# Attention step: all value units of a batch in one run at its end, twelve buffers of exponentials, heads set singly between half projections

## The reference

```python
Q = layernorm(x) @ Wq.T + bq; K = ctx @ Wk.T + bk; V = ctx @ Wv.T + bv
scores = softmax(einsum('bhsd,bhtd->bhst', Q, K) / sqrt(16))
x = x + tanh(g_xattn) * (einsum('bhst,bhtd->bhsd', scores, V) @ Wh.T + bh)
x = x + tanh(g_ffn) * moe_ffn(layernorm(x))   # 8 experts, best 2, low-rank updates, F = 1024
```

## Time and profile before

| what | us |
|---|---|
| median of 3 runs | 541.9 |
| the runs | 544.21, 534.79, 541.9 |
| profiled execution | 535.67 |
| its span, first to last instruction | 533.9 |
| PE busy | 505.6 (95%) |
| DVE, POOL, ACT busy | 355.7, 291.2, 257.9 |
| granted PE clock, mean | 0.99 |

### The profile page before, as it was taken

How to read it: one execution, slowest core, us unless ns; L and a number is a source line. 1 busy time by engine, 2 the same in 40 slices (tenths; PEclk the granted TensorE clock), 3 DMA queues, 4 the chain that set the end, 5 groups by cost and what they waited for, 6 DMA issues and landing times.

```text
span 533.9 us, 11800 instructions
## 1 busy us (share of the span) xinstructions
PE 505.6 (95%) x4358; PEld 460.0 (86%) x4358; DVE 355.7 (67%) x774; ACT 257.9 (48%) x576; POOL 291.2 (55%) x335
## 2 busy tenths in 40 slices
PE   3788999999999999999998999999999999999995
PEld 2576888888888888888788999999999999999993
DVE  6866677777777777887766777765475555754443
ACT  2556565555555555556767523453335334343331
POOL 5552566655554566552559955744367433844441
PEclk9989999999999999999999989999999999999998
DMA  7575687667677777764111000001000100001000
GB/s 212 142 251 123 197 209 151 168 156 161 165 163 169 177 186 190 163 141 110 24 18 15 2 1 1 2 1 31 2 1 1 32 0 1 2 0 32 0 1 31
DMA packets 51287, 45.83 MB, mean 86 GB/s; under 512 B 34295, under 2 KB 40703, under 8 KB 51231
## 3 DMA queue, kind: packets, MB, share of 16 engines
q1 hardware_dynamic: 41324, 21.03, 16.9%
q0 software_dynamic: 6560, 15.83, 12.4%
q10 hardware_dynamic: 3346, 8.23, 5.3%
HBM read 20.59 MB, written 6.66 MB: 51 GB/s over the span
## 4 chain that ended last, share of the span: by engine, by line
PE 80%; DVE 6%; DMA 6%; ACT 2%; SPq 2%; issue 1%; POOL 1%; ACTq 0%; POOLq 0%; DVEq 0%
PE bank L1293 13%; PE bank L1155 9%; PE bank L1185 7%; PE bank L1172 7%; PE bank L1345 6%; PE bank L1297 6%; PE bank L1310 6%; PE bank L1132 5%; PE bank L1140 5%; PE bank L1325 4%; DMA QS<-crow 4%; PE bank L1218 2%; PE bank L1328 2%; DVE nmax L911 2%; PE bank L1259 2%; PE bank L1247 2%
## 5 line engine op out<-in xcount | busy, mean ns | idle before, releaser
L911 DVE TENSOR_REDUCE nmax<-bank 100x1 f32<-100x361 f32 x256 | 128.0, 527 | 52.8 <-PE bank L1155 49.4
L400 POOL TENSOR_TENSOR awl<-hb,awh 128x400 fp32r<-128x400 f32 x64 | 71.2, 1114 | 102.3 <-ACT awh L604 102.3
L509 ACT ACTIVATE pt<-bank 120x400 f32<-120x400 f32 (+1 forms) x192 | 82.7, 505 | 24.2 <-PE bank L1172 23.8
L1155 PE MATMUL bank<-KS,QS 96*100 96x362 f32 x256 | 88.8, 383 | 4.9 <-DVE nmax L911 3.1
L850 DVE TENSOR_TENSOR hb<-sil,bank 128x400 f32<-128x400 f32 x64 | 36.5, 570 | 83.4 <-PE bank L1310 39.1
L604 ACT ACTIVATE awh<-hb 128x400 fp32r<-128x400 f32 x64 | 34.5, 539 | 118.9 <-DVE hb L857 118.6
L343 POOL DMA_DIRECT2D KS<-kn x64 | 33.2, 526 | 90.6 <-PE bank L1155 56.2
L1155 PEld LDWEIGHTS bank<-KS,QS 96*100 96x100 f32 x256 | 42.0, 167 | 23.9 <-issue 13.4
L1172 PE MATMUL bank<-QS,KS 97*120 97x200 f32 (+1 forms) x384 | 50.8, 268 | 2.7 <-DVE qn L760 1.6
L1172 PEld LDWEIGHTS bank<-QS,KS 97*120 97x120 f32 (+1 forms) x384 | 48.9, 185 | 4.9 <-DMA QS<-crow 2.8
L333 POOL DMA_DIRECT2D QS<-q_dram x90 | 46.2, 526 | 6.4 <-DMA q_dram<-qn 6.4
(11 more groups left out here) (178 smaller groups left out, 1123.9 us busy)
## 6 DMA issues: line engine op xcount, KB each, us to landing
KS<-kn SPq DMA_DIRECT2D x128, 90.5 KB, 2.9
KS<-kn POOLq DMA_DIRECT2D x64, 90.5 KB, 2.7
craw<-ctxT POOLq DMA_DIRECT2D x14, 361.0 KB, 5.5
QS<-q_dram POOLq DMA_DIRECT2D x92, 50.0 KB, 5.1
q_dram<-qn ACTq DMA_DIRECT2D x4, 400.0 KB, 4.9
o_dram<-on SPq DMA_DIRECT2D x16, 100.0 KB
xr<-o_dram SPq DMA_DIRECT2D x16, 100.0 KB
y<-xs SPq DMA_DIRECT2D x16, 100.0 KB
```

The costliest lines, as they stand in the source:

```text
L400: nc.gpsimd.tensor_tensor(awl[:, g % 2, slot], hb[:, slot], awh[:, g % 2, slot].bitcast(F32), ALU.subtract).then_inc(m["p_awl"], 1)
L509: nc.scalar.activation(pt[0:TW[t], u % 6, :], pT[u % 3][0:TW[t], 0:CS], ACT.Exp, scale=float(DH) ** -0.5).then_inc(m["act_e"], 1)
L911: nc.vector.tensor_reduce(nmax[:, pos:pos + 1], pS[h % 2][0:S, 0:T], AX.X, ALU.max, negate=True).then_inc(m["dve_s"], 1)
L1155: mm(pS[h % 2][0:S, 0:TP], QS[b % 3][0:96, g, h % 2, j, :], KS[b % 3][0:96, g, j, :], start=True, stop=True).then_inc(m["pe_s"], 1)
```

## The change

- PE: in steps 0 to 14 the twelve value units of batch i come in one run at the end of step i, behind head 15; step 15 keeps its four visits. The visit behind scores 0 to 2 is gone.
- pt has twelve buffers (UN = 12) instead of six; exponential u waits for value unit u of the batch before.
- PE: k_proj and v_proj are cut into halves of three matmuls, with one head between the halves, where heads stood in pairs.
- ACT: row_out(i, 1) goes between exponentials 1 and 2, k_high(b, 0) ahead of the copy of the sums, row_out(i + 1, 0) between exponentials 7 and 8.
- DVE: k_low(b, 0) goes from behind head 4 to behind head 3, k_low(b, 1) from ahead of head 8 to behind it; ctx_high, the small operations root and head 14 move by a place.

```diff
-        pt = sba("pt", [121, 6, CS])
+        pt = sba("pt", [121, UN, CS])
...
-                wait(act, "pe_pv", n - 5)
-                nc.scalar.activation(pt[0:TW[t], u % 6, :], pT[u % 3][0:TW[t], 0:CS], ACT.Exp,
+                wait(act, "pe_pv", n - UN + 1)
+                nc.scalar.activation(pt[0:TW[t], u, :], pT[u % 3][0:TW[t], 0:CS], ACT.Exp,
...
                     expo(i, 1)
+                    row_out(i, 1)
                     expo(i, 2)
+                if has_k(i):
+                    k_high(b, 0)
                 if has_o(i):
                     wait(act, "pe_pv", i * UN)
...
                     head(i + 1, 7)
+                    head(i + 1, 8)
                 if has_k(i):
                     k_low(b, 1)
-                if i in (11, 12):
-                    root(0, 7 * (i - 11) + 2)
-                if has_s(i):
-                    head(i + 1, 8)
...
+            def k_part(b, j, p0, p1):
+                for p in range(p0, p1):
+                    (hw, hc), k = TERMS[p // KT], p % KT
+                    last = mm(pP[(1, 0)[j]][:, 0:TP], wkv[:, 0, hw, k, j * 128:(j + 1) * 128],
+                              cth[:, b % 2, hc, k, :], start=p == 0, stop=p == 5)
+                if p1 == 6:
+                    last.then_inc(m["pe_k"], 1)
...
                     st_unit(i, 2)
-                if has_o(i):
-                    pv_unit(i - 1, 9)
-                    pv_unit(i - 1, 10)
-                    pv_unit(i - 1, 11)
                 if has_s(i):
                     s_head(i + 1, 0)
-                    s_head(i + 1, 1)
...
-                    k_proj(b, 0)
+                    pe.wait_ge(m["ctx_l"], b + 1)
+                    k_part(b, 0, 0, 3)
+                if has_s(i):
+                    s_head(i + 1, 1)
+                if has_k(i):
+                    k_part(b, 0, 3, 6)
                 if has_s(i):
                     s_head(i + 1, 2)
+                if has_k(i):
+                    wait(pe, "act_c", 2 * i + 2)
+                    v_part(b, 0, 0, 3)
+                if has_s(i):
                     s_head(i + 1, 3)
                 if has_k(i):
-                    wait(pe, "act_c", 2 * i + 2)
-                    v_proj(b, 0)
+                    v_part(b, 0, 3, 6)
                 if has_s(i):
                     s_head(i + 1, 4)
...
                     s_head(i + 1, 9)
                 if has_k(i):
                     wait(pe, "dve_kl", KT * b + 2)
-                    v_proj(b, 1)
+                    v_part(b, 1, 0, 3)
                 if has_s(i):
                     s_head(i + 1, 10)
+                if has_k(i):
+                    v_part(b, 1, 3, 6)
...
+                if has_s(i):
+                    s_head(i + 1, 14)
                 if has_y(i):
                     y_proj(i)
                 if has_s(i):
-                    s_head(i + 1, 14)
                     s_head(i + 1, 15)
+                    pv_unit(i, 0)
+                    pv_unit(i, 1)
...
+                    pv_unit(i, 11)
```

More of the change, by code:

```diff
@@ L649, in body @@
                     expo(i, 7)
+                if has_s(i):
+                    row_out(i + 1, 0)
+                if has_u(i):
                     expo(i, 8)
@@ L653, in body @@
                     w_high(5)
-                if has_s(i):
-                    row_out(i + 1, 0)
                 if has_k(i):
@@ L973, in body @@
                     head(i + 1, 2)
-                    head(i + 1, 3)
                 if i in (11, 12):
@@ L977, in body @@
                 if has_s(i):
-                    head(i + 1, 4)
+                    head(i + 1, 3)
                 if has_k(i):
                     k_low(b, 0)
+                if has_s(i):
+                    head(i + 1, 4)
+                if i in (11, 12):
+                    root(0, 7 * (i - 11) + 2)
                 if has_s(i):
@@ L1023, in body @@
                     head(i + 1, 12)
-                    head(i + 1, 13)
                 if i in (11, 12):
                     root(0, 7 * (i - 11) + 5)
+                if has_s(i):
+                    head(i + 1, 13)
+                    head(i + 1, 14)
                 if i == 1:
@@ L1039, in body @@
                 if has_s(i):
-                    head(i + 1, 14)
                     head(i + 1, 15)
@@ L1129, in k_proj, with v_part @@
                     pe.wait_ge(m["ctx_l"], b + 1)
-                for n, (hw, hc) in enumerate(TERMS):
-                    for k in range(KT):
-                        last = mm(pP[(1, 0)[j]][:, 0:TP], wkv[:, 0, hw, k, j * 128:(j + 1) * 128],
-                                  cth[:, b % 2, hc, k, :], start=n + k == 0, stop=n + k == 3)
-                last.then_inc(m["pe_k"], 1)
+                k_part(b, j, 0, 6)
+            def k_part(b, j, p0, p1):
[5 more added lines that the diff above has]
+                    last.then_inc(m["pe_k"], 1)
             def v_proj(b, t):
+                v_part(b, t, 0, 6)
+            def v_part(b, t, p0, p1):
                 bank = pP[1] if b < 2 and t == 1 else pP[0]
-                for n, (hw, hc) in enumerate(TERMS):
-                    for k in range(KT):
-                        last = mm(bank[0:TW[t], 0:D], cth[:, b % 2, hc, k, T0[t]:T0[t] + TW[t]],
-                                  wkv[:, 1, hw, k, :], start=n + k == 0, stop=n + k == 3)
-                last.then_inc(m["pe_v"], 1)
+                for p in range(p0, p1):
+                    (hw, hc), k = TERMS[p // KT], p % KT
+                    last = mm(bank[0:TW[t], 0:D], cth[:, b % 2, hc, k, T0[t]:T0[t] + TW[t]],
+                              wkv[:, 1, hw, k, :], start=p == 0, stop=p == 5)
+                if p1 == 6:
+                    last.then_inc(m["pe_v"], 1)
             def s_head(b, h):
@@ L1422, in body @@
                 b = i + 2
-                if has_u(i):
-                    st_unit(i, 0)
-                    st_unit(i, 1)
-                    st_unit(i, 2)
-                if has_o(i):
-                    pv_unit(i - 1, 9)
-                    pv_unit(i - 1, 10)
-                    pv_unit(i - 1, 11)
+                st_unit(i, 0)
+                st_unit(i, 1)
+                st_unit(i, 2)
                 if has_s(i):
                     s_head(i + 1, 0)
-                    s_head(i + 1, 1)
-                if has_u(i):
-                    wait(pe, "act_v", min(NT * (i + 2), NT * B))
-                    wait(pe, "act_c", 2 * i)
-                    row_turn(i, 1)
-                    if i == B - 1:
-                        gate(0)
+                wait(pe, "act_v", min(NT * (i + 2), NT * B))
+                wait(pe, "act_c", 2 * i)
+                row_turn(i, 1)
+                if i == B - 1:
+                    gate(0)
                 if has_k(i):
@@ L1469, in body @@
                     u_proj(0)
+                if has_k(i):
+                    wait(pe, "act_v", NT * b + 1)
+                    k_part(b, 1, 0, 3)
                 if has_s(i):
@@ L1472, in body @@
                 if has_k(i):
-                    wait(pe, "act_v", NT * b + 1)
-                    k_proj(b, 1)
+                    k_part(b, 1, 3, 6)
                 if i == B - 2:
@@ L1519, in body @@
                     wait(pe, "act_v", NT * b + 2)
-                    v_proj(b, 2)
+                    v_part(b, 2, 0, 3)
                 if has_s(i):
                     s_head(i + 1, 13)
+                if has_k(i):
+                    v_part(b, 2, 3, 6)
+                if has_s(i):
+                    s_head(i + 1, 14)
                 if has_y(i):
@@ L1525, in body @@
                 if has_s(i):
-                    s_head(i + 1, 14)
                     s_head(i + 1, 15)
+                    pv_unit(i, 0)
+                    pv_unit(i, 1)
+                    pv_unit(i, 2)
+                    pv_unit(i, 3)
+                    pv_unit(i, 4)
+                    pv_unit(i, 5)
+                    pv_unit(i, 6)
+                    pv_unit(i, 7)
+                    pv_unit(i, 8)
+                    pv_unit(i, 9)
+                    pv_unit(i, 10)
+                    pv_unit(i, 11)
             for i in range(0, B):
```

41 lines of the change are left out of this document (20 added, 21 removed).

## The result

The change made the kernel slower: a median of 554.59 us in 4 runs (551.36 to 558.62) against 538.39 us for the kernel before in 4 runs (534.79 to 544.21), a ratio of 1.030 with a 95% interval of 1.0245 to 1.0349. The forecast was 536, its range 521 to 550. The profiled execution took 553.36 us, with a span of 551.5 (before: 535.67 and 533.9). My sum had given 532.0 for it, so 21.4 us are missing.

A forecast was written before the change was run, and what follows sets the result against it. PE's own issue time was taken to bound the step: 14.61 - 1.08 + 1.03 = 14.56 us. Together -3.7 us gave 532.0 for the profiled execution; between medians of 532 and 538 the forecast was 536, range 521 to 550.

The forecast's parts named there:

- (d): Store of the row maxima ahead of scores unit 6: taken as landing in time, 0 us, bounds 0 and +1.4 us.
- step 0 at +0.5: First attention step: three visits become a burst, a wait is added and a DVE hole goes, +0.5 us in all.
- (e): Roots in steps 11 and 12, row_out and osb copy change places on engines with slack: 0.3 us for the roots.
- the clock at 1.00: TensorE's granted clock in steps 0 to 14, read from the earlier trace as 1.00, the full 2.4 GHz.
- (a): One visit to the value units for four, in each step: 3.47 us become 2.4, saving 1.08 us a step.
- R3: Rival: a visit's price goes with its units, or 192 records outpace what feeds PE; 544 us, chance 0.1.
- (b): Halves of projections with one head between, on PE: no cost taken, bounds +-0.3 us a step.
- (c): New DVE order: PE waits for the low half of k before the second v projection, 1.03 us in steps 0 to 13.
- R1: Rival: the wait for the low half of k doesn't bite; steps of 13.5 us, 518 to 524 us, chance 0.2.
- way of 0.42 us: PE's time from head 8's matmul to the second v projection before the change, without the visit's tail: 0.42 us.
- R2: Rival: the row store still lands late; 12 to 18 us if in thirteen steps, 544 to 550 us; chance 0.2.
- base of 541.9: Median of the kernel before's runs used by the forecast: 541.9 us, 6.2 us above the profiled execution.

The follow-up runs named there:

- all three repairs: Changed kernel with DVE's low half of k back ahead of head 8, roots 4 and 11 ahead of the context cast, xr load behind the row store: 532.83 us, 0.988.
- the kernel before with two repairs: Kernel before with the xr load behind the row store of step 0 and two roots ahead of the context cast in steps 11 and 12: 535.68 us, 0.989.
- the single repairs: Three runs of the changed kernel, one edit each: low half of k ahead of head 8, 537.81 us; roots ahead of context cast, 546.17; xr load behind store, 546.72.

## Why the prediction was wrong

The undisturbed step was right. What failed are terms beside it that were put at nothing or nearly so: the store at 0 us (d), step 0 at +0.5, the roots at 0.3 (e), and the clock at 1.00. Of the 21.3 us of span above my sum, the holes for the store and the roots are 2.42 + 2.15 + 4.52 = 9.1 us. Half clock is up to 7.9 us by an estimate from the window rows (PE was busy for 15.7 of the 17.0 us at 0.50, and half of that is lost). 2.5 us lie outside the stage, and the rest is spread.

**(a), the burst: right.** 2.4 us were forecast for twelve units, with entry and exit; 2.2 us stand between its start and the next scores. The saving of 1.08 us a step was 0.9 under the new order. R3 is out. What I had not seen is that it holds only with that order; in the old one 0.3 us is left. At first I had read a visit as pure cost, since PE goes on without a hole; but DVE was working under it (the rows of the burst alone show PE waiting for it in its place), and the earlier trace rows had shown DVE busy in three quarters of the time.

**(b), single heads: right within its bounds.** A head between two half projections takes 0.17 to 0.18 us (188.31 to 188.48, 195.35 to 195.53).

**(c), the wait for the low half of k: right in mechanism, place and size.** 1.46 us from head 8 to the v projection against 1.45 forecast, and the third group of the step takes 3.34 us where the sum had 3.08 - 0.81 + 1.03 = 3.30. R1 is out, and the step comes to 14.67 against 14.56. Only the way of 0.42 us without the wait was too short: undoing the order gives back 0.62 us and leaves 0.77, so R1's step of 13.5 us wasn't to be had.

**(d), the store at 0 us: wrong, and R2 was right on it in some steps.** The distance, 6.01 us, was right. Landings of 5.08, 5.47 and 5.36 us cost 0.50, 0.87 and 0.78 us in steps 2, 6 and 8, or 2.1 us. R2's price for late landings in thirteen steps, 12 to 18 us, did not come, so the result above 550 doesn't speak for R2. I had argued that the cause moves away, because the loads of q end earlier. They do, by 0.8 us in step 9: GpSimd has issued them 2.2 us into the step and not 3.0. But the store moves with them, from 2.6 to 1.5 us into the step, so that they end 0.64 us behind its issue where they ended 0.35 us behind it. By its semaphore in the traces it landed after 2.6 to 5.5 us in steps 1 to 11, and after 4.6 to 6.0 before: the moves helped, but not in every step, and the slack of 4.5 us is short by what is left. The Trainium skill, "DMA: Bandwidth & Descriptors", Queues, rings and completion order, says that each DMA engine takes turns between the queue rows, packet by packet. That a small store then waits for its own row and little else was my inference from it, and the rows don't bear it out: alone in ACT's queue the store landed after 5.41 us.

**Step 0 at +0.5 us: wrong, it was +6.0.** The row that I cited for it, 0.29 us for the store at 52.65, was the warning: nothing of the store's lateness could move, since it is issued when those four loads have landed, while PE arrives earlier by as much as the new order shortens the way (from 6.5 to 5.7 us of the step). Each tenth that PE saves ahead of it is a tenth of hole. The store was also issued 0.9 us later than before. With the store ahead of xr the hole and the half clock went together, and of the 6.0 us gained only 2.42 were the hole. The repair isn't sure: with all three repairs step 0 had a hole of 1.60 us again.

**(e), the roots at 0.3 us: wrong, and the dearest of the steps for its size.** It said that items of under 0.3 us change places on engines with slack. Two of them became 2.5 us each. The two holes are 4.5 us, with the half clock 6.6 us in steps 11 and 12, of which moving one root a step gave back 4.0. It could have been read: the root of 1.55 us at 218.57, beside others of 0.15, was in the trace of before. The Trainium skill, "SBUF — State Buffer", section Who interferes with whom, says that a DVE instruction with two SBUF inputs contends with a GpSimd instruction that reads SBUF, and that issue order decides who blocks. The common end at 229.5 agrees with the first. With the second the rows don't agree: the root starts at 227.00, 0.7 us before line 328, when GpSimd is still issuing transfers, and does not end before line 328 does.

**The clock was not in the forecast at all.** I took 1.00 as given because the earlier trace rows showed it. Half clock followed holes, and by the estimate above cost nearly as much as those for the store and the roots. When a hole draws it and when not is open: the hole of 2.26 us at 248.93 and the 0.78 and 0.88 us in step 8 did not, 0.87 us twice in step 6 did, and the kernel before with two repairs had a hole of 1.04 us and full clock throughout steps 0 to 14. No run tells how much of the 33 us that the single repairs gave, against 21.8 together, is the place where it happened to fall.

**The median.** The profiled execution lies 1.2 us below the median of the change, and the base of 541.9 came down to 538.4 with one more run. Neither matters beside 21 us. About 2.5 us of these lie outside steps 0 to 14; half clock at 390.8 and 452.2, where the kernel before has none, fits them but was not tested.

## What to carry to other kernels

A step's sum on the engine that bounds it can be right to 0.1 us and the sum of the whole still be off by 4%. Check apart the first step, whose loads end at a fixed time, and each step with extra work; look for every instruction whose duration in the trace is several times that of its like, ask what ran beside it, and do this for each item that the change moves. A visit that seems to cost PE time may be another engine's time to catch up, and a wait that a repair takes away must be looked for again under the next semaphore.

## What the runs showed of the hardware

- A DVE instruction with two SBUF inputs on 100 x 8 numbers took 0.15 us alone and 1.54, 1.55, 1.78, 1.80, 2.49 and 2.50 us beside GpSimd's subtraction of 128 x 724, each time ending 0.02 to 0.04 us behind it (kernel before, change, roots moved).
- After holes in PE of 0.9 to 4.4 us in a stage where it is otherwise busy for over 90%, the granted clock fell to 0.50 for 3.4, 6.8 or 10.2 us in some cases and stayed at 1.00 in others: none fell behind 2.26 us at 248.93 in the change, 1.60 us in step 0 with three repairs, or 1.0 to 1.1 us in the repaired old order and with the weight load in mid step. The kernel before, whose longest hole behind the first unit of these steps is 0.65 us, has no half clock there.
- A store of 3.1 KB took 4.6 to 6.0 us to land in steps 1 to 11 of the kernel before, where six loads of 50 KB and one of 361 KB were issued within some 4 us of it; 2.6 to 5.5 us in the change; 5.41 us from ACT's queue in step 0; 2.0 to 4.4 us when GpSimd's loads came later; and 1.8 us in steps 12 to 14 of the change, where no context load is left and the loads of q are issued earlier or not at all.
- A visit to the value units cost PE 0.80 to 0.84 us at three places of a step, for six bundles of 0.09; four visits in one cost 2.2.
